# Cross-attention and FFN: the mask of heads 8 to 15 moved from TensorE to VectorE, their maximum subtracted on GpSimd, and a new order of all queues

## The reference

```python
def layernorm(x): return (x - mean(x)) / sqrt(var(x) + 1e-5)
q = layernorm(x) @ Wq.T; k = ctx @ Wk.T; v = ctx @ Wv.T       # split into 16 heads of 32
logits = where(mask == 0, -1e9, (q @ k^T) / sqrt(32))         # 77 keys per head
x = x + (softmax(logits) @ v) merged @ Wo.T
s = layernorm(x) @ Win + bin_                                 # 64 columns
g = einsum(relu(s[..., None] * W1 + b1), W2) + b2             # 64 x 16 inner units
out = x + g @ Wout + bout
```

## Time and profile before

| | |
|---|---|
| three executions | 942.89, 941.86, 945.23 us; median 942.89 |
| the profiled execution | 940.78 us; its span from first to last instruction 939.1 us |
| mean granted TensorE clock | 0.905 of full speed |
| busy share of the span | TensorE 85%, VectorE 71%, ScalarE 57%, GpSimd 57% |
| DMA share of 16 engines, 160 to 760 us | 0.60 to 0.71 |

### The profile page before, as it was taken

The page is one execution under the profiler, slowest core; times in us unless marked ns, Lnnn a source line. Parts: engine busy times, 40 slices in busy tenths (PEclk is TensorE's granted clock), DMA queues, the critical chain, the costliest instruction groups (busy, mean ns, idle before and its releaser), DMA issues.

```text
span 939.1 us, 16984 instructions
## 1 busy us (share of the span) xinstructions
PE 796.4 (85%) x5778; PEld 377.8 (40%) x5778; DVE 664.4 (71%) x1199; ACT 535.2 (57%) x835; POOL 530.8 (57%) x500
## 2 busy tenths in 40 slices
PE   6865788989979796989989896979899798988666
PEld 5433344443535252434435352444435353534121
DVE  1337687787868686786878785887868687878322
ACT  3354547565665746665665656575666658565512
POOL 6034576756574756656575755666575657565510
PEclk9977889998989897999989897999989898999876
DMA  9413473747766575747576565837476566353711
GB/s 335 114 45 80 100 145 74 152 119 162 147 119 149 124 175 97 166 95 175 123 140 148 122 165 102 163 96 163 123 146 144 123 163 121 72 132 77 140 45 68
DMA packets 329111, 120.90 MB, mean 129 GB/s; under 512 B 316783, under 2 KB 317447, under 8 KB 329019
## 3 DMA queue, kind: packets, MB, share of 16 engines
q1 hardware_dynamic: 328443, 119.09, 57.3%
q10 hardware_dynamic: 576, 0.64, 0.2%
HBM read 22.64 MB, written 16.78 MB: 42 GB/s over the span
## 4 chain that ended last, share of the span: by engine, by line
PE 72%; DVE 10%; ACT 5%; issue 5%; POOL 3%; DMA 3%; SPq 0%; ACTq 0%; POOLq 0%; DVEq 0%
PE tr_banks L1582 17%; PE mm_banks L1582 17%; PE lg_banks L1619 9%; PE mm_banks L1637 7%; PE mm_banks L1683 5%; PE mm_banks L1694 4%; PE lg_banks L1616 3%; ACT inner L955 3%; PE tr_banks L1674 3%; PE mm_banks L1692 2%; DVE qT L1262 2%; PE mm_banks L1574 1%; POOL p_parts L719 1%; DVE probs L1277 1%; DVE row_max L1273 1%
## 5 line engine op out<-in xcount | busy, mean ns | idle before, releaser
L719 POOL TENSOR_TENSOR p_parts<-probs,p_parts 128x616 f16<-128x616 f32 x128 | 172.0, 1355 | 70.0 <-ACT p_parts L935 69.8
L1582 PE MATMUL tr_banks<-xT,wqT 128*128 128x512 f16 x768 | 179.7, 386 | 6.6 <-DMA xT<-x_parts 5.4
L713 POOL TENSOR_TENSOR probs<-probs,row_inv 128x616 f32<-128x616 f32 x128 | 154.3, 1217 | 48.1 <-DVE row_inv L1293 48.1
L1582 PE MATMUL mm_banks<-woT,aT 128*128 128x512 f16 x768 | 171.0, 379 | 1.3 <-DVE aT L1299 0.6
L1619 PE MATMUL lg_banks<-k_blocks,qT 128*128 128x308 f16 x768 | 152.4, 316 | 0.0
L1273 DVE TENSOR_REDUCE row_max<-lg_banks 128x8 f32<-128x616 f32 x128 | 100.8, 787 | 65.6 <-PE lg_banks L1619 65.2
L935 ACT ACTIVATE p_parts<-probs 128x616 f16<-128x616 f32 x128 | 90.5, 712 | 62.8 <-POOL probs L713 56.8
L1277 DVE TENSOR_TENSOR probs<-lg_banks,row_max 128x616 f32<-128x616 f32 x128 | 102.4, 800 | 29.7 <-POOL p_parts L719 19.1
L927 ACT ACTIVATE probs<-probs 128x616 f32<-128x616 f32 x128 | 90.9, 713 | 51.3 <-DVE probs L1277 50.1
L1674 PE MATMUL tr_banks<-s_parts,spread 128*128 128x512 f16 x128 | 58.7, 479 | 70.0 <-ACT inner L955 35.2
L1582 PEld LDWEIGHTS tr_banks<-xT,wqT 128*128 128x128 f16 x768 | 73.7, 99 | 107.4 <-issue 26.3
(11 more groups left out here) (96 smaller groups left out, 995.7 us busy)
## 6 DMA issues: line engine op xcount, KB each, us to landing
xr<-in_x SPq DMA_DIRECT2D x32, 512.0 KB, 4.6
out_x<-xr SPq DMA_DIRECT2D x32, 512.0 KB, 3.1
v_now<-v_blocks SPq DMA_DIRECT2D x6, 384.0 KB, 2.9
pT<-p_parts SPq DMA_TRANSPOSE x128, 3.6
k_blocks<-kT_all SPq DMA_DIRECT2D x32, 38.5 KB, 2.5
pT<-in_L_xattn_Wk SPq DMA_DIRECT2D x1, 1024.0 KB, 8.9
wq_raw<-in_L_xattn_Wq SPq DMA_DIRECT2D x1, 1024.0 KB, 12.9
qT<-in_L_xattn_Wv SPq DMA_DIRECT2D x1, 1024.0 KB, 15.1
```

Of the source, the lines that this page charges most:

```text
L713: pool.tensor_tensor(block_of(k), block_of(k), inv, ALU.mult).then_inc(probs_ready, 1)
L719: pool.tensor_tensor(p_parts[:, k % PS, 1, 0:2 * LW], probs[:, k % 4, :], p_parts[:, k % PS, 0, 0:2 * LW], ALU.subtract).then_inc(p_lowere ...
L1582: last = pe.matmul(bank, stationary(a, c), moving(b, c), start=(n == 0), stop=(n == len(passes) - 1))
```

## The change

Odd halves (heads 8 to 15) get their mask on VectorE: it adds the mask to the logits on the way from PSUM to SBUF, reduces the maximum there, and GpSimd subtracts it. Even halves stay as they were. `max_done` and `shifted` become a pair of semaphores each, and a new one, `masked`, tells TensorE that an odd half has left PSUM. `ffn_weights` moves from step -1 into step 0. All written-out orders are new.

```diff
 def maxima(step, k):                                   # VectorE
-    dve.tensor_reduce(top, logits, AX.X, ALU.max).then_inc(max_done, 1)
+    if k % 2 == 0:
+        dve.tensor_reduce(top, logits, AX.X, ALU.max).then_inc(max_done[0], 1)
     if not (isinstance(n, int) and n < 4):
         dve.wait_ge(p_lowered, n - 3)
-    dve.wait_ge(max_done, n + 1)
-    dve.tensor_tensor(probs_of(k), logits, top..., ALU.subtract).then_inc(shifted, 1)
+    if k % 2 == 0:
+        dve.wait_ge(max_done[0], m)
+        dve.tensor_tensor(probs_of(k), logits, top..., ALU.subtract).then_inc(shifted[0], 1)
+    else:
+        dve.tensor_tensor(probs_of(k), logits, mask_bias[:, g.slot, k // 2, :]..., ALU.add).then_inc(masked, 1)
+        dve.wait_ge(masked, m)
+        dve.tensor_reduce(top, probs_of(k), AX.X, ALU.max).then_inc(max_done[1], 1)
+def subtract(step, k):                                 # GpSimd, new
+    pool.wait_ge(max_done[1], T * g.n + k // 2 + 1)
+    pool.tensor_tensor(block_of(k), block_of(k), top..., ALU.subtract).then_inc(shifted[1], 1)
 def exps(step, k):                                     # ScalarE
-    act.wait_ge(shifted, n + 1)
+    act.wait_ge(shifted[k % 2], T * g.n + k // 2 + 1)
 def logits(step, k):                                   # TensorE; u = k % 2
-    pe.wait_ge(shifted, n - 1)
+    u == 0: pe.wait_ge(shifted[0], ...)   u == 1: pe.wait_ge(masked, ...)
-        pe.matmul(bank, ident16, mask_bias..., start=True, stop=False)
+        if u == 0: pe.matmul(bank, ident16, mask_bias..., start=True, stop=False)
```

More of the change, by code:

```diff
@@ L557, in fill_step @@
                     turn_x(step, 1)
+                if soft:
+                    place_wout(step)
+                if ahead:
                     turn_x(step, 2)
@@ L560, in fill_step @@
                     turn_h(step, 0)
+                    turn_h(step, 1)
                 if ahead:
@@ L563, in fill_step @@
                 if soft:
-                    turn_h(step, 1)
+                    next_values(step)
+                if late:
+                    place_values(step)
             def loop_step(step):
@@ L625, in drain_step @@
                 if ffn:
-                    store(step, 0)
                     store(step, 1)
+                    reload(step, 1)
                 if soft:
@@ L1022, in fill_step @@
                 if soft:
+                    exps(step, 6)
                     h_normal(step, 0)
@@ L1097, in loop_step @@
                     exps(step, 6)
+                if ahead:
+                    x_part(step, 2)
+                if soft:
+                    exps(step, 7)
                 if back:
@@ L1356, in fill_step @@
                     maxima(step, 0)
-                    maxima(step, 1)
-                    sums(step, 0)
-                    maxima(step, 2)
+                if ahead:
+                    x_statistics(step, 0)
                 if late:
@@ L1422, in loop_step @@
                 if soft:
+                    sums(step, 0)
+                if front:
+                    q_low(step, 0)
+                if soft:
                     sums(step, 1)
@@ L1428, in loop_step @@
                     maxima(step, 4)
-                    maxima(step, 5)
-                if front:
-                    q_low(step, 0)
+                if ahead:
+                    x_statistics(step, 0)
+                    x_statistics(step, 1)
+                    x_counted(step)
                 if back:
@@ L1498, in drain_step @@
                     h_means(step, 1)
+                if ffn:
+                    output(step, 1)
+                if front:
+                    q_low(step, 2)
                 if soft:
@@ L1502, in drain_step @@
                     a_low(step, 0, 1)
-                    maxima(step, 7)
+                if ffn:
+                    output(step, 2)
+                if soft:
                     sums(step, 2)
                     residual(step, 0)
+                    maxima(step, 7)
                     residual(step, 1)
                     h_counted(step, 0)
-                if front:
-                    q_low(step, 2)
+                if back:
+                    s_low(step)
                 if soft:
@@ L1514, in drain_step @@
                 if ffn:
-                    output(step, 1)
-                if back:
-                    s_low(step)
-                if ffn:
-                    output(step, 2)
                     output(step, 3)
@@ L1718, in fill_step @@
                     logits(step, 4)
+                if late:
+                    late_wo(step)
                 if front:
@@ L1725, in fill_step @@
                     q(step, 2)
+                if soft:
+                    logits(step, 6)
+                if front:
                     q(step, 3)
@@ L1739, in loop_step @@
                 if ffn:
-                    ffn_pre(step, 4)
-                    ffn_g(step, 0)
                     ffn_pre(step, 5)
@@ L1748, in loop_step @@
                     ffn_g(step, 4)
-                if front:
-                    q(step, 0)
+                if soft:
+                    logits(step, 2)
                 if ffn:
@@ L1761, in loop_step @@
                     q(step, 1)
+                if soft:
+                    logits(step, 4)
                 if back:
@@ L1764, in loop_step @@
                     pv(step, 1, 1)
+                if front:
+                    q(step, 2)
                 if soft:
-                    logits(step, 4)
                     logits(step, 5)
@@ L1783, in loop_step @@
                     ffn_in(step)
-                if soft:
-                    logits(step, 7)
-                if back:
                     ffn_pre(step, 0)
@@ L1826, in drain_step @@
                 if back:
+                    pv(step, 1, 0)
+                    pv(step, 1, 1)
+                if front:
+                    q(step, 1)
+                if ffn:
+                    ffn_out(step, 0)
+                if back:
                     wo(step, 2)
                     wo(step, 3)
-                if soft:
-                    logits(step, 6)
+                if ffn:
+                    ffn_out(step, 1)
                 if front:
@@ L1836, in drain_step @@
                     logits(step, 7)
+                if ffn:
+                    ffn_out(step, 2)
+                if soft:
                     wo(step, 0)
                     wo(step, 1)
+                if back:
+                    ffn_in(step)
                 if front:
```

450 lines of the change are left out of this document (226 added, 224 removed).

## The result

The changed kernel takes 953.99 us (median of five runs, 950.98 to 955.0) against 942.89 (941.44 to 945.66): a ratio of 1.0104, 95% interval 1.0075 to 1.0132. It is slower by about 1%. That lies inside the range of 928 to 957, but the forecast was 942, with a chance of 0.40 for faster, 0.27 for no change and 0.33 for slower. The profiled executions have spans of 952.5 and 939.1, a difference of 13.4.

What follows compares the result with a forecast made beforehand. TensorE was taken as the bound, except in a sparse part of each step that is a chain of waits. Twelve steps +2.2, fill -2.2 and drain -1 gave -1.0 on 942.89, so 942 us; range 928 to 957.

Steps and rivals of the forecast that it cites:

- the terms of the dense part: From `q(0)` or `logits(2)` to the next step, TensorE never idle before: three added costs, +0.55, +0.25 and +0.93 us per step.
- +0.55 before `ffn_out(0)`: TensorE waits for `g_copy` and `g_low`, which `logits(2)` covers only partly where `q(0)` did fully; us per step.
- +0.25 for the logits: Dense part: five masked logits halves (5.25 us) become six halves, three without mask (5.5 us), per step.
- +0.93 before `wo(0)`: TensorE waits for `a_low(0,1)`, since only `logits(7)` covers it now; us per step, bounds 0.2 to 1.3.
- the sparse part: Step's first 17 us, a half-clock chain of waits: `logits(0)` leaves it, `relus(4)` starts earlier; -1.55 us per step (-0.7 to -2.2).
- The pauses at the three loop turns keep their place, after `ffn_pre(3)`: nothing.: Hardware loop's turns: TensorE's pauses stay where they were in the order, so no cost was counted.
- Net -2.2: Fill: us gained in total, as `pv(0,0)` comes about 2.3 earlier but `place_wout` moves before `turn_x(2)`; bounds 0 to -6.
- The 6.49: Fill: TensorE's wait in us for VectorE before `logits(2)`, expected to go as the FFN split leaves its place ahead of `maxima(0)`.
- the turned half 0 comes at the same time: Fill, SyncE: `place_rest` takes `place_wout`'s place before `turn_p(0)` and lasts about as long, 10.30 against 11.17 us, so no delay.
- The drain's -1: Kernel's end: us gained in total, two subtractions before div(0) set against earlier sums and `ffn_out` in waits; bounds -4 to +3.
- The faster one: Rival: full clock returns before `ffn_g(0)` and the wait before `wo(0)` shrinks; -1.0 us per step, 928 us; chance 0.28.
- The slower one: Rival: GpSimd's chain to `pv(0,0)`, slack 1.5 us, comes late as VectorE's scaling is held; 950 to 957 us; chance 0.25.

Runs made afterwards that it cites:

- e6: The changed kernel with 16 extra small transposes in TensorE's setup, results unread; 948.30 us, ratio 1.0081 to the kernel before.
- e11: The changed kernel with 4 extra small transposes in TensorE's setup, results unread; 947.95 us in its one run.
- e5: The kernel before, unchanged, run once more for a second trace; 943.84 us in its one run.
- e10: The kernel before with 16 extra small transposes in TensorE's setup; 938.61 us, ratio 0.9987 to the kernel before.
- e7: The changed kernel with `logits(6)` moved behind `pv(0,1)` and `logits(7)` behind `ffn_in`, their followers later too; 947.97 us, ratio 1.0073 to the kernel before.
- e8: The changed kernel with `logits(3)` moved ahead of `ffn_out(0)`; 944.54 us, ratio 1.0044 to the kernel before.
- e12: e9 with `h_normal(2)` ahead of `a_part`, `h_means(1)` ahead of `maxima(5)` and `q_low(1)` ahead of `residual(2)`; 931.81 us, ratio 0.9918 to the kernel before.
- e4: The changed kernel with `logits(0)` back ahead of `ffn_pre(4)` and `ffn_g(0)`; 958.83 us, ratio 1.0189 to the kernel before.
- e9: The changed kernel with the edits of e6, e7 and e8 together; 940.54 us, ratio 0.9999 to the kernel before.
- e3: The changed kernel with the fill lists of the kernel before, FFN split in step -1; 953.08 us, ratio 1.0125 to the kernel before.

## Why the prediction was wrong

**Right: the terms of the dense part.** +0.55 before `ffn_out(0)`, +0.25 for the logits and +0.93 before `wo(0)` make 1.73; dense grew from 33.83 to 35.56, 1.73. The two waits are 0.57 and 0.96 in the step shown, with the releasers that were named. (Three slips in the working change nothing: 8 x 0.13 is 1.04; 57% of 51 and 4.8 make 34 and not 37, while the loop of after shows 36; and the two rows of L1290 lie in one step.)

**Right ahead of the turns, too large behind them: the sparse part.** The mean is -1.33 instead of -1.55. In the four steps ahead of the first turn it is -1.6 to -1.8, so the mechanism was right; in the six behind a turn it is -0.3 to -1.6. What differs is the clock. `relus(4)` comes nearly as forecast in all of them, but `logits(0)` now stands between it and `ffn_pre(5)`, in the step shown partly at half clock: 486.16 to 487.73. `relus(5)` therefore waits until 488.14, and the forecast had counted only up to `relus(4)`. Ahead of the first turn the clock is back 11.0 to 11.9 after T0 and `relus(5)` starts at 12.4 to 12.8; in the first step behind a turn the clock is back at 13.5 and 13.8 and `relus(5)` starts at 13.7 and 13.8, so the gain there is 0.3 and 0.95 (sparse 16.94 and 17.03, before 17.28 and 17.98). Two windows of after, in the step from 422.58, whose clock is back at 436.0:

```profile
434.00:436.00 2.00, 2.00 (x9) 1.16 (x8) 0.02 (x1) 1.26 (x2) 0.66 (x1) 0.50 0.95 217
436.00:438.00 2.00, 2.00 (x14) 0.96 (x13) 1.90 (x3) 1.69 (x3) 2.00 (x3) 0.99 0.92 178
```

With this the step is +0.41 instead of +0.18, twelve of them +4.9 instead of +2.2; ahead of the first turn it is +0.02.

**The failed step: "The pauses at the three loop turns keep their place, after `ffn_pre(3)`: nothing."** The first pause kept its length, 3.85 for 4.28, and stands close to its old place in the order, yet the turns cost +5.7, the largest term of all, and the steps behind them are those that lose. A second pause appeared, and e6 and e11 show that it hangs on where the code lies; the time at half clock behind it is its larger part. Without it, e6 loses 9.0 at its turns, before 8.7. The forecast priced the turn by the order of work alone and left no bound for it.

**A term that two traces can't price: the fill, "Net -2.2".** The 6.49 went as said. In the trace of after "the turned half 0 comes at the same time" did not hold: `place_rest` begins only at 82.62, `turn_p(0)` 1.4 later than in before once more, and `pv` pays for the wait with half clock; against that execution the start is +1.45. But eight kernels with the mechanism have these fill lists. Take from each start its key multiplications, which nothing edits: before has 144.9 to 145.5 in its three traces (before, e5, e10); of the eight, five have 145.9 to 146.9 (after, e6, e7, e8, e12) and three 143.3 to 143.7 (e4, e9, e11), which is 1.2 to 2.2 below before, nearly as forecast. In the three, TensorE waits 1.5 to 1.7 for pT and `pv` runs at full clock, in the five 3.0 to 3.2 and partly at half. TensorE of e11:

```profile
98.10 2.15 PE L1683 MATMUL mm_banks<-pT,v_now 128*32 128x256 f16 x72 [1.49 <-DMA pT<-p_parts]
101.73 5.34 PE L1625 MATMUL mm_banks<-woT,aT 128*128 128x512 f16 x24 [1.48 <-DVE aT L1337]
```

e11 differs from after by four transposes alone, so the +1.45 is not a price of the lists. In the old fill order the mechanism costs some +2.6 (e3's 159.04 against 156.43; the key multiplications take 10.8 and 10.9 in these two). The drain's -1 had no worked sum, and came as -1.55; before's own end was 160.6, 160.6 and, in e10, 157.4, so this shows nothing either way.

**The rivals.** The faster one, a clock of 1.0 before `ffn_g(0)`, is refuted: that stretch is at 0.50 in after too (484 to 486 in the step shown). The slower one gave the right side and, with 950 to 957, the right time, but not its mechanism, so that the measured time lies in the stated range is luck: `pv(0,0)` starts at 517.76 without idle, straight behind `q(3)`; e7 starts it 0.9 earlier without a wait for pT. Its premise, that VectorE's scaling would be held by a running GpSimd operation, came otherwise: more of the 64 are held (40 take over 0.25 us, before 32), but shorter (2 over 0.9 us, before 29), and the mean fell from 600 ns (line L1290 in the groups of before) to 461. The kernel before:

```profile
L1290 DVE TENSOR_SCALAR row_sum<-row_sum 128x16 f32<-128x16 f32 x64 | 38.4, 600 | 2.2
```

The Trainium skill, "SBUF — State Buffer", section "Who interferes with whom", has reductions as free of this contention. The trace agrees: the maximum from SBUF, next to a GpSimd that is busy 64% of the span, takes 794 to 796 ns in all its 64 executions.

Counted together, between the traces of after and of before once more: 4.9 (steps) + 5.7 (turns) + 1.45 (start) - 1.55 (end) = 10.5 us; forecast were 2.2 + 0 - 2.2 - 1 = -1.0. Of the 11.5 between them, 5.7 are the turns, 3.7 the fill, 2.7 the sparse part, and -0.6 the end. The turns' term goes with the second pause in every trace; those of the fill and the end lie within what start and end vary by.

## What to carry to other kernels

Where work is moved out of a stretch in which it covered a handover, the handover's price can be counted from rows to a tenth of a microsecond, and a line such as e8's, which puts other work in its place, gives it back. A transfer of work to another engine is an order problem first: the same mechanism saved 0.58 us per step in one order and cost 3.6% in another. At the turns of a hardware loop read the pauses of the new trace themselves before any cause in the order is sought; they can move with the code. And a stage that runs once, such as the fill, is not priced by one trace of each kernel.
